# Gated linear attention on one core: Pool's query scaling and log gates in eight operations each

## The reference, cut to what matters

```python
q = _l2norm((h @ Wq).reshape(B, T, N_HEADS, D_K))
k = _l2norm((h @ Wk).reshape(B, T, N_HEADS, D_K))
v = (h @ Wv).reshape(B, T, N_HEADS, D_V)
alpha = jax.nn.sigmoid(h @ Wg).reshape(B, T, N_HEADS, D_K)
...
S = a_t[..., None] * S + k_t[..., None] * v_t[..., None, :]
o_t = jnp.einsum('bhkv,bhk->bhv', S, q_t)
```

## Time and profile before

| | us |
|---|---|
| median of 3 runs | 2762.19 |
| range of them | 2758.3 to 2762.64 |
| the profiled execution | 2774.5 |
| its span, first to last instruction | 2772.7 |
| PE busy over the span | 2133.4 (77%) |
| DVE busy | 1794.6 (65%) |
| ACT busy | 1330.4 (48%) |
| Pool busy | 1220.9 (44%) |
| the 722.6 us from 87.4 to 810 us: PE / DVE / ACT / Pool busy | 654.8 / 554.7 / 409.2 / 304.2 |

### The profile page before, as it was taken

The page is one execution under the profiler, slowest core; times in us unless marked ns, Lnnn a source line. Parts: engine busy times, 40 slices in busy tenths (PEclk is TensorE's granted clock), DMA queues, the critical chain, the costliest instruction groups (busy, mean ns, idle before and its releaser), DMA issues. The chain is left out here.

```text
span 2772.7 us, 47493 instructions
## 1 busy us (share of the span) xinstructions
PE 2133.4 (77%) x15968; PEld 1480.9 (53%) x15968; DVE 1794.6 (65%) x4213; ACT 1330.4 (48%) x2849; POOL 1220.9 (44%) x1099
## 2 busy tenths in 40 slices
PE   2799889898979688059299996859999999852780
PEld 0466566665668467047245554745556666541560
DVE  3678777777766756211467773848988889847113
ACT  2565646465634247023245554736666666620223
POOL 2453535344411000735422212557877778710663
PEclk9899999999999567579679998979999999965785
DMA  6400000000001000122333331000000000000113
GB/s 200 107 1 2 2 2 1 2 2 1 1 17 53 0 0 1 49 57 67 92 95 84 81 103 52 0 0 1 0 0 0 0 0 0 0 31 0 44 44 95
DMA packets 103467, 89.44 MB, mean 32 GB/s; under 512 B 12060, under 2 KB 90166, under 8 KB 103222
## 3 DMA queue, kind: packets, MB, share of 16 engines
q1 hardware_dynamic: 96150, 72.67, 9.5%
q0 software_dynamic: 7168, 14.73, 1.7%
HBM read 59.02 MB, written 40.96 MB: 36 GB/s over the span
## 5 line engine op out<-in xcount | busy, mean ns | idle before, releaser
L3264 POOL TENSOR_SCALAR mb_w<-mb_duT,mb_bT 128x256 f32<-128x256 f32 x512 | 467.9, 933 | 116.8 <-PE bank L3274 85.4
L3199 DVE TENSOR_TENSOR_SCAN mb_hs<-mb_dA,bank 128x512 f32<-128x512 f32 x256 | 301.0, 1206 | 34.6 <-issue 24.9
L3293 PE MATMUL bank<-mb_hc,ident 128*128 128x512 f32 x512 | 256.1, 624 | 15.7 <-DVE mb_hc L3209 15.4
L38 POOL TENSOR_TENSOR scrap<-ones 128x1 f32<-128x1 f32 x64 | 12.5, 195 | 575.4 <-DVE gla_ss L390 365.5
L3255 ACT ACTIVATE mb_dA<-mb_delta,mb_A 128x255 f32<-128x255 f32 x512 | 217.2, 498 | 8.4 <-DVE mb_hs L3199 8.2
L2421 DVE TENSOR_REDUCE ra_mx<-bank 128x2 f32<-128x512 f32 x256 | 163.9, 687 | 59.7 <-PE bank L2275 57.2
L2003 ACT ACTIVATE e_hid<-bank,e_b 128x512 f32<-128x512 f32 (+1 forms) x128 | 79.1, 635 | 256.0 <-PE bank L2047 178.0
L2511 ACT ACTIVATE ra_pT<-bank 128x512 f32<-128x512 f32 x256 | 141.2, 600 | 112.9 <-PE bank L2297 112.7
L3274 PE MATMUL bank<-ident,mb_w 128*128 128x128 f32 x1024 | 150.0, 280 | 34.4 <-DVE mb_hs L3199 26.3
L502 DVE TENSOR_TENSOR gla_mid<-bank,gla_ex 128x512 f32<-128x512 f32 x128 | 88.3, 690 | 128.4 <-ACT gla_ex L490 128.4
L518 DVE COPY_PREDICATED gla_sT<-c_seen,bank 128x768 f32<-128x768 int32 x128 | 130.1, 1017 | 36.5 <-issue 36.5
(11 more groups left out here) (538 smaller groups left out, 5684.4 us busy)
## 6 DMA issues: line engine op xcount, KB each, us to landing
results<-const_empty SPq DMA_DIRECT2D x2, 4096.0 KB
e_got<-results SPq DMA_DIRECT2D x32, 256.0 KB, 3.3
rope_rows<-ra_part SPq DMA_DIRECT2D x48, 128.0 KB, 1.9
ra_k<-rope_rows SPq DMA_DIRECT2D x32, 192.0 KB, 3.2
ra_q<-rope_rows SPq DMA_DIRECT2D x32, 192.0 KB, 4.3
queue<-const_spare_rows SPq DMA_DIRECT2D x1, 4128.0 KB
e_x<-queue SPq DMA_DIRECT2D x8, 516.0 KB
e_w<-in_L_ffn_w SPq DMA_DIRECT2D x2, 2048.0 KB, 8.1
```

Source lines behind the costliest of these rows:

```text
L3199: dve.tensor_tensor_scan(hs[n // 2 % 2][:, n % 2, :, :].rearrange("p c t -> p (c t)"), dA[n % RD][:, :, :].rearrange("p c t -> p (c t)"), ...
L3264: ins = pool.tensor_scalar(w[n % RH][:, h, :], duT[k][:, h, :], bT[k][:, h, n:n + 1], None, ALU.mult)
L3293: ins = pe.matmul(YB[:, :], g.ident[:, :], hc[grp % 2][:, j, :, :].rearrange("p c t -> p (c t)"), start=(n == 0), stop=(n == NS - 1))
```

## The change

Pool's two query operations become eight, one for each pair of heads (256 elements in each partition), and its one log gate operation becomes eight likewise. Each counts its semaphore up by one. PE's transposes of a pair wait for the pair's own query piece, and its sums for the pair's own log gate piece. ACT gets a wait ahead of the first gate item of a sequence: all eight log gate pieces of the sequence before must have read the tile `az` that it is about to write.

```diff
@@ act_item
         if kind == "z":
+            if c == 0 and not first(s):
+                act.wait_ge(lna_ready, at(s - 1, HP - 1))
             act.wait_ge(z_psum, s * 4 + (c + 1))
@@ pe_project
         if hp == 0:
             pe.wait_ge(ktok_ready, s * 4 + 4)
-            pe.wait_ge(qs_ready, s * 2 + 1)
-        if hp == 2:
-            pe.wait_ge(qs_ready, s * 2 + 2)
+        pe.wait_ge(qs_ready, at(s, hp))
...
-        if hp == 0:
-            pe.wait_ge(lna_ready, s + 1)
+        pe.wait_ge(lna_ready, at(s, hp))
@@ gpsimd
             def scaled_queries(s, k):
                 pool.wait_ge(rnq_ready, s + 1)
-                for heads in (slice(0, 4), slice(4, HEADS)):
-                    n = heads.stop - heads.start
-                    rows = tok["q"][k][:, :, heads.start * DK:heads.stop * DK].rearrange("p t (h d) -> p t h d", d=DK)
-                    pool.tensor_tensor(rows, rows, rnq[:, :, heads].unsqueeze(3).broadcast_to([P, 2, n, DK]), ALU.mult)\
-                        .then_inc(qs_ready, 1)
+                for hp in range(HP):
+                    rows = tok["q"][k][:, :, hp * P:(hp + 1) * P].rearrange("p t (h d) -> p t h d", d=DK)
+                    pool.tensor_tensor(rows, rows, rnq[:, :, 2 * hp:2 * hp + 2].unsqueeze(3).broadcast_to([P, 2, 2, DK]),
+                                       ALU.mult).then_inc(qs_ready, 1)
 
             def log_gates(s, k):
                 pool.wait_ge(zl_ready, s + 1)
                 pool.wait_ge(zm_ready, s * 4 + 4)
-                pool.tensor_tensor(lna[k], lna[k], az[:, :, :], ALU.subtract).then_inc(lna_ready, 1)
+                for hp in range(HP):
+                    ch = slice(hp * P, (hp + 1) * P)
+                    pool.tensor_tensor(lna[k][:, :, ch], lna[k][:, :, ch], az[:, :, ch], ALU.subtract).then_inc(lna_ready, 1)
```

## The result

| | before | after |
|---|---|---|
| median of 4 runs, us | 2760.99 | 2726.27 |
| range, us | 2758.3 to 2762.64 | 2717.2 to 2735.08 |
| ratio | | 0.9875, 95% interval 0.9841 to 0.9909 |
| profiled execution, us | 2774.5 | 2726.4 |

The changed kernel is 1.25% faster; the forecast was 2730 us, 1.2% less. I read its profile in the same order as before the change.

The account below looks back on a forecast made before the run. PE was busiest, its step 7 gap waiting for DVE, held by Pool's long operations. DVE's stalls 26 + opening 2 + clock 4 - added waits 0 = 32 us; 2762.2 - 32 = 2730 us, range 2714 to 2756.

Parts of the forecast that it names:

- What bounds the block, and which stall counts: Changed block: PE's 2.03 us wait in step 7 is DVE's; ACT ends step 6, which stays at 6.15 us.
- DVE's stalls: DVE's products in steps 5 and 6 wait for shorter Pool pieces: 1.75 us gained a sequence, 26 us (16 to 34).
- Pool's time: Pool's pieces per sequence: eight query pieces 4.6 us for 3.8, eight log gate pieces 5.5 for 4.5; costs nothing.
- The opening: Sequence 0: first sum starts 2.9 us earlier, partly lost to DVE meeting Pool's pieces; 2 us gained (0 to 2.9).
- The clock: Step 7 behind PE's gap: three stretches at TensorE's 1.2 GHz level go; 4 us gained (0 to 10).
- The added waits: PE's 13 more waits a sequence, 208 in all, at L427 and L435: cost 0, upper bound 10 us.
- behind the last: Rival at DVE's products: DVE gets in only after Pool's last piece; 2790 us, slower; 8%.
- The gain was not taken back: Rival: step 7 shortens but what follows waits for something unseen; about 5 of 32 us stay, 2757 us; 9%.
- The full gain: Rival: neither DVE product meets a piece for long and the slow stretches vanish; 46 us gained, 2716 us; 13%.

## Why the prediction was right

**What bounds the block, and which stall counts.** Right. Step 7 lost what DVE's products lost, step 6 nothing: the gap of 0.84 us turned into a longer wait for ACT. The runs with one half cut and the one without the logarithm show each part.

**DVE's stalls.** The forecast for step 6's products was 0.70 and 0.88 us, measured 0.83 and 0.94; for the gap of `v3` 0.2, measured 0.29; for step 7 a gain of 1.75, measured 6.88 - 5.15 = 1.73 in most sequences and 1.65 in the first three. 15 x 1.7 = 26 us. I had step 6 at 6.15 us still; it grew by 0.06 to 0.07 in twelve sequences, 0.8 us in all.

**Pool's time.** Query pieces took 0.61 us alone (forecast 0.61), eight of them 4.62 us in the opening (4.6) and 4.99 beside DVE's products. Eight log gate pieces took 5.88 us, where I had 5.5 and the hold-ups by DVE on top. Nothing waited for them.

**The opening.** Forecast 2 us, measured 1.4: the first sum came as forecast (79.3, measured 79.49), but a third DVE instruction, L412, which was not in my sum, also got slower (1.00 us for 0.60 before). I had read the hold as one of products of two tiles alone. By step 2 of that sequence the lead is 2.1 us.

**The clock.** This was the term that was too small. Before, six of the steps 7 that don't stand at a turn of the loop held a stretch at the lower level and lasted 7.92 to 8.43 us instead of 6.88, 8.1 us in all. After, none does: those that are to be read whole last 5.15 or 5.23. I had taken 4 us. The steps 0, where such stretches stand too, moved both ways: two behind a turn of the loop fell from 8.3 to 6.8, another rose from 8.3 to 9.3, and so did the first behind the opening, from 7.5 to 8.5. In all, the steps 7 gave 34.4 us (26.2 and 8.1), the first sequence up to its step 2 gave 2.1, the other steps 0 gave 1.6, and the steps 6 took 0.8: 37.3 of the block's 37.7 us. How many slow stretches would go was a guess, which no row decided; that the median came within 4 us of the forecast all the same is in part luck.

**The added waits.** Nothing, as taken.

**The rivals.** DVE got in behind each piece, not behind the last. The gain was not taken back. The full gain did not come with the change, since the products still meet a piece each; it came with the run that keeps the pieces away from them.

## What to carry to other kernels

Before cutting an engine's work into pieces, look at who stands beside it: here nobody needed the results earlier, and the gain came from an instruction on another engine that got in between the pieces. Piece size is no virtue by itself: by the length of step 7, two pieces were a little better than four, and four pieces ahead of the product and four behind it better than eight in a row. And a stall is priced at the next wait of the engine that sets the end: of 5.9 us that DVE stood in a sequence, 2.56 and 0.78 counted only by what they delayed on Pool.

## What I had not expected of the hardware

- A Pool operation with one input tile of 2048 elements (5.38 us) held DVE's product only until 3.9 us after its start; those with two inputs held it to their end + 0.29 us. Why the hold ends early there is open. A power on 32 elements (5.46 us) held nothing. A row of Pool's duration alone doesn't tell how long it holds DVE.
- The second of two items that is held up costs 0.26 us more than its gap (1.02 + 1.12 for 1.88 us).
- TensorE's lower clock (a granted clock of 0.51 in the earlier trace rows) went from all the steps 7 that lost their 2 us gap, the turns of the loop aside, and in the run with Pool's one-input operation a gap of 1.40 us in the same place brought none either. The new gap of 1.54 us ahead of the transposes, just one step earlier, brought none into step 7. With the gap of 2.03 us six of ten steps 7 held one and four didn't; why those is open.
